# Row statistics of x1 made once in the first node stage of a graph network kernel, and gathered as two table columns

## The chip, the cores and the metric

The kernel runs on one core of a Trainium2 chip. The metric is the device time of one execution in microseconds (us), the median of several runs. PE is the matrix engine, DVE the vector engine, ACT the scalar engine, POOL GpSimd, and SP the engine whose queue issues most DMA transfers.

## The reference, cut to what matters

Four graph layers work on x (10000 x 512) and 5000 edges. The first two, cut to the lines around the change:

```python
def _layernorm(x, axis=-1, eps=1e-05):
    m = jnp.mean(x, axis=axis, keepdims=True)
    v = jnp.var(x, axis=axis, keepdims=True)
    return (x - m) / jnp.sqrt(v + eps)
...
h = jnp.maximum(_layernorm(x, axis=-1), 0.0)
x = x + _L0_gnn_ref(h, ...)      # this x is the kernel's x1
h = jnp.maximum(_layernorm(x, axis=-1), 0.0)
x = x + _L1_gnn_ref(h, edge_index, edge_type_8, edge_weight, ...)
...
# _L0_gnn_ref, node part
z = jnp.concatenate([x, agg], axis=1)
return jax.nn.relu(z @ W3 + b3) @ W4 + b4
...
# _L1_gnn_ref, message part
h = (x @ W.T).reshape(n, h_, d_)
e_src = jnp.einsum('ehd,hd->eh', h[src], a_src)
e_dst = jnp.einsum('ehd,hd->eh', h[dst], a_dst)
```

## The kernel before, in words

The program runs its stages one after the other, each in a block of its own, and each stage's tiles have a letter: prepare (a), layer 0's edges (b), **layer 0's nodes (c)**, **layer 1's messages (d)**, softmax (s) and sums (e), **layer 1's nodes (n)**, and so on up to layer 3's edges (h). Tables in HBM pass the results on; x1 is one, 512 columns wide (its name in the trace is x). A tile has 128 rows, a group four tiles.

**First node stage, c (layer0_nodes).** Ten rounds of two groups, b = 0 and 1. The trace has it from about 948 to 1640 us, a round in some 66 us. Per round: PE turns the normalised rows of X into c_tp_ps; ACT copies them out (c_hTh, L928) and DVE makes the rest of the split (c_hTl, L976). PE multiplies with W3 (c_u_ps); DVE adds the gathered sums (L993, c_U); PE turns that (L1037); ACT applies bias and relu (c_R at L935, c_zh at L936), and DVE subtracts them for c_zl (L983), five chunks per group. PE multiplies with W4 (c_o_ps), and DVE adds the result to the residual in XB (L1003). Each engine's order is written out by hand as one program. While one round runs, the next round's X is loaded (L831) and its statistics made (L963); the residual x is loaded into XB (L841); POOL gathers the sums of edges (L898) and adds the bias b4 to XB in two instructions of 128 x 2048 (L903). The store of XB into x1 (L845) waits for the last addition of its group. SP's queue in a round is: two loads of X, two residual loads, each of which waits for the store of its half of XB a round ago, two stores.

**Messages, d (layer1_messages).** From about 1640 to 1909 us. Ten groups of 4 x 128 edges, each with a source row and a destination row of x1, gathered by POOL into d_X, eight gathers a group (L1160), one group ahead. DVE makes the statistics (L1239, L1246, L1248, L1250), with the root on ACT (L1179), ACT applies them with relu (L86), and PE turns the rows (L1323). ACT and DVE split them (L1195, L1258), PE multiplies with W (d_m_ps) and with the projection of the attention vectors (d_proj_ps), and ACT and DVE copy the messages out (L1199, L1263). The projections' operand is made at the stage's start (L1310).

**Second node stage, n (layer1_nodes).** From about 2034 to 2413 us, ten rounds like c's, without PE: it loads x1 (n_X), makes its statistics on DVE (L1687), adds x1's own rows and the gathered sums (L1708, L1734, L1741), and POOL adds a bias (L1643) and gathers (L1632).

Of the kernel before, what the change touches and what calls it, by code (L numbers as in the profile page):

```python
# [37 lines left out]
EPS = 1e-5  # L38
XW = F + 4
# [751 lines left out]
def layer0_nodes(nc, core, a, keep, T0, x1):  # L791
# [10 lines left out]
    o_ready, o_out = sem("c_o"), sem("c_oout")  # L802
    stored = [sem("c_st0"), sem("c_st1")]
# [3 lines left out]
    with ExitStack() as st:  # L807
        sb = lambda n, s, d=F32: core.sb(st, "c_" + n, s, d)
        X = sb("X", [P, 2, GROUP, F])
        XB = sb("XB", [P, 2, GROUP, F])  # L810
        G = sb("G", [P, 2, GROUP, IN])
        idx = sb("idx", [P, GT], I32)
        stt = core.stats(st, "c")
        hTh, hTl = sb("hTh", [P, 2, KF, GROUP * P], F32R), sb("hTl", [P, 2, KF, GROUP * P], F32R)
# [12 lines left out]
        with nc.Block() as block:  # L827
            @block.sync
            def _(sp):
# [3 lines left out]
                def load_last(buf, b, sems):  # L833

                    for p, n in LAST:
                        at = (NG - 1) * GROUP * P + p * GROUP
                        sp.dma_start(buf[p:p + n, b, :, :], a["x"][at:at + n * GROUP, :].rearrange("(p j) f -> p j f", p=n)
                                     ).then_inc(sems[b], 16)
# [47 lines left out]
            def _(pool):  # L886
# [5 lines left out]
                def round_(r, late):  # L892
# [8 lines left out]
                    for b in range(2):  # L901
                        pool.wait_ge(res_loaded[b], r * 16 + (16 + late * b))
                        pool.tensor_tensor(XB[:, b, :, :], XB[:, b, :, :], over(b4[:, :].unsqueeze(1), [P, GROUP, F]),  # L903
# [10 lines left out]
            def _(act):  # L914
                def root(r):
                    act.wait_ge(var_ready, r * GT + GT)
                    layer_norm_std(act, stt, keep["eps"]).then_inc(std_ready, 1)
                    act.wait_ge(norm_ready, r + 1)

# [24 lines left out]
                with act.Fori(0, NR) as r:  # L944
# [7 lines left out]
                    for j in range(GROUP):  # L952
                        turned_rows(r + 1, (2 * j, 2 * j + 1))

            @block.vector
            def _(dve):
# [41 lines left out]
                def add_residual(r, b, j):  # L998
# [4 lines left out]
                    dve.tensor_tensor(XB[:, b, j, :], o[:, t % 2, :], XB[:, b, j, :], ALU.add).then_inc(o_out, 1)  # L1003

                def round_(r, late):
# [6 lines left out]
                    for j in range(GROUP):  # L1012
# [87 lines left out]
def layer1_messages(nc, core, a, keep, x1, msg, logit):  # L1100
# [5 lines left out]
    x_loaded = [sem("d_x0"), sem("d_x1")]  # L1106
    ln_step, var_ready, std_ready, norm_ready, h_ready = (sem("d_" + n) for n in ("lnstep", "var", "std", "norm", "h"))
# [6 lines left out]
    with ExitStack() as st:  # L1114
        sb = lambda n, s, d=F32: core.sb(st, "d_" + n, s, d)
        X = sb("X", [P, 2, 2, GROUP, F])
        idx = sb("idx", [P, 2, 2 * GROUP], I32)
        stt = core.stats(st, "d")
# [4 lines left out]
        Wraw, Wrow = X[:, 1, 0, :, :], X[:, 1, 1, :, :]  # L1123
# [10 lines left out]
        with nc.Block() as block:  # L1134
# [12 lines left out]
            def _(pool):  # L1147
                pool.memset(diag[:, :, :, :], 0.0).then_inc(diag_set, 1)

                def gather(g, b, before, turned):  # L1150
                    pool.wait_ge(x_loaded[b], before)
# [7 lines left out]
                    for i in range(2 * GROUP):  # L1159
                        pool.indirect_dma_start(X[:, b, i // GROUP, i % GROUP, :], None, x1[:, :],  # L1160
                                                bass.IndirectOffsetOnAxis(idx[:, b, i:i + 1], 0),
                                                bounds_check=ROWS_N - 1, oob_is_err=False).then_inc(x_loaded[b], 16)
# [4 lines left out]
                with pool.Fori(0, ER) as r:  # L1167
                    gather(r * 2 + 1, 1, r * 128, r * 16)
                    gather(r * 2 + 2, 0, r * 128 + 128, r * 16 + 8)
                pool.wait_ge(x_loaded[0], 128 * (ER + 1))  # L1170
                pool.wait_ge(x_loaded[1], 128 * ER)
# [3 lines left out]
            def _(act):  # L1175
                def root(g, q):
                    n = slice(GROUP * q, GROUP * q + GROUP)
                    act.wait_ge(var_ready, g * 8 + (4 * q + 4))
                    act.activation(stt["std"][:, n], stt["mv"][:, n, 1], ACT.Sqrt, bias=keep["eps"][:, 0:1]).then_inc(std_ready, 1)  # L1179

                def norm_rows(g, b, q, rows):
                    act.wait_ge(norm_ready, g * 2 + (q + 1))
                    for j in rows:
                        x = X[:, b, q, j, :]
                        relu_norm(act, x, x, stt, GROUP * q + j).then_inc(h_ready, 1)
# [16 lines left out]
                for q in range(2):  # L1202
                    root(0, q)
# [1468 lines left out]
```

## Time and profile before

| | us |
|---|---|
| median of 3 runs | 3022.01 (3018.73 to 3023.68) |
| span of the profiled execution | 3096.9 |
| first node stage (c) in it | about 948 to 1640 |
| message stage (d) in it | about 1640 to 1909 |
| second node stage (n) in it | about 2034 to 2413 |

No other time of the profiled execution is given; its span is 74.9 us longer than the median.

Rows of the timeline read: start, duration, engine, line, operation, tile written <- tiles read, shapes, how many of them in a row, and in brackets the idle time before them with what ended it. SPq is the issue of a DMA by SP's queue. Rows of stretches read: the stretch, its length, busy time (and instructions) of PE, PE's weight loads, DVE, ACT, POOL, then the granted PE clock (1.00 is 2.4 GHz, 0.50 is 1.2 GHz), the busy share of the DMA engines and GB/s. Rows of waits read: who waited for whom, us in total, how often, the longest.

### The profile page before, as it was taken

Reading aid. Unit: us, or ns where it says so; the run is one execution under the profiler, and the core shown is the slowest. Engines: PE = TensorE matmul, PEld = TensorE weight load, DVE = VectorE, ACT = ScalarE, POOL = GpSimd, SP = SyncE. Lnnn points to the kernel's source line nnn. Section 1 sums busy time; section 2 is a strip of 40 time slices with the busy share of each in tenths; the row PEclk is TensorE's granted clock in tenths of the full one; section 3 lists DMA queues with packets and bytes.
Section 4 is the critical chain, followed back from the end, with each engine's and each line's share of the span. In section 5 each row is a group of like instructions: output and inputs, shape, how many; then the busy total and the mean of one; then the engine's idle time right before and its main releaser. Section 6 shows DMA issues by size and latency. Waiting matters only on the chain. (4 is left out here: it accounts for less than half of the span.)

```text
span 3096.9 us, 40519 instructions
## 1 busy us (share of the span) xinstructions
PE 2274.6 (73%) x13127; PEld 2008.0 (65%) x13127; DVE 1744.5 (56%) x3459; ACT 1089.9 (35%) x1842; POOL 970.3 (31%) x762
## 2 busy tenths in 40 slices
PE   6989999999995999999996996510000165899466
PEld 6979898989895888888885875410000154777355
DVE  4633232323234544445443657879999367999444
ACT  2234333333343343333332554323333263333232
POOL 1001010000003322232313341655665504565565
PEclk9989999999997999999997998765555577999778
DMA  6101010101023232322323231234432534665443
GB/s 200 34 8 55 18 51 17 51 17 50 20 49 145 103 114 95 142 114 94 98 90 123 82 96 42 92 144 146 149 133 101 174 127 178 245 245 222 141 139 119
DMA packets 111202, 330.20 MB, mean 107 GB/s; under 512 B 25980, under 2 KB 39292, under 8 KB 90570
## 3 DMA queue, kind: packets, MB, share of 16 engines
q1 hardware_dynamic: 61628, 228.63, 19.6%
q0 software_dynamic: 42976, 99.20, 10.9%
q10 hardware_dynamic: 6530, 1.53, 0.2%
q8 instruction: 36, 0.59, 0.1%
q14 instruction: 32, 0.26, 0.0%
HBM read 247.80 MB, written 128.41 MB: 121 GB/s over the span
## 5 line engine op out<-in xcount | busy, mean ns | idle before, releaser
L1914 PE MATMUL f_c_ps<-f_zeros 128*40 128x258 f32 x4 | 1.9, 641 | 389.2 <-DVE f_heads L1369 389.2
L1914 PEld LDWEIGHTS f_c_ps<-f_zeros 128*40 128x40 f32 x4 | 0.6, 174 | 390.2 <-DVE f_heads L1369 389.7
L135 PE MATMUL b_y_ps<-W23h,b_Rh 128*128 128x320 f32 x800 | 249.7, 312 | 0.0
L136 PE MATMUL b_y_ps<-W23l,b_Rh 128*128 128x320 f32 x800 | 246.4, 308 | 0.6 <-issue 0.6
L137 PE MATMUL b_y_ps<-W23h,b_Rl 128*128 128x320 f32 x800 | 246.6, 308 | 0.2 <-issue 0.2
L536 POOL DMA_INDIRECT b_X<-in_x,b_idx x40 | 40.3, 1008 | 635.0 <-PE b_tp_ps L716 624.4
L135 PE MATMUL b_hid_ps<-b_hTh,W1h 128*128 128x512 f32 x500 | 201.4, 403 | 7.9 <-ACT b_Rh L585 7.9
L135 PE MATMUL c_u_ps<-c_W3h,c_hTh 128*128 128x320 f32 x640 | 201.2, 314 | 0.0
L136 PE MATMUL b_hid_ps<-b_hTl,W1h 128*128 128x512 f32 x500 | 200.2, 400 | 0.0
L137 PE MATMUL b_hid_ps<-b_hTh,W1l 128*128 128x512 f32 x500 | 200.0, 400 | 0.0
L137 PE MATMUL c_u_ps<-c_W3h,c_hTl 128*128 128x320 f32 x640 | 198.0, 309 | 0.0
L136 PE MATMUL c_u_ps<-c_W3l,c_hTh 128*128 128x320 f32 x640 | 197.9, 309 | 0.0
L903 POOL TENSOR_TENSOR c_XB<-c_XB,c_b 128x2048 f32<-128x2048 f32 x20 | 92.0, 4617 | 325.9 <-DMA c_XB<-in_x 325.9
L650 DVE TENSOR_TENSOR b_Rl<-b_R,b_Rh 128x512 fp32r<-128x512 f32 x100 | 69.2, 692 | 220.8 <-ACT b_Rh L585 220.8
L935 ACT ACTIVATE c_R<-c_tp_ps,c_b 128x512 f32<-128x512 f32 x100 | 68.8, 688 | 305.4 <-PE c_tp_ps L1037 297.4
L135 PE MATMUL c_o_ps<-c_W4h,c_zh 128*128 128x512 f32 x400 | 162.2, 405 | 3.8 <-DVE c_zl L983 3.7
L675 DVE TENSOR_TENSOR b_Yl<-b_y_ps,b_Yh 128x320 fp32r<-128x320 f32 x80 | 39.3, 492 | 216.1 <-ACT b_Yh L597 212.5
L137 PE MATMUL c_o_ps<-c_W4h,c_zl 128*128 128x512 f32 x400 | 156.8, 392 | 0.0
L136 PE MATMUL c_o_ps<-c_W4l,c_zh 128*128 128x512 f32 x400 | 156.3, 391 | 0.0
L137 PEld LDWEIGHTS b_y_ps<-W23h,b_Rl 128*128 128x128 f32 x800 | 150.1, 188 | 1.2 <-issue 1.2
L136 PEld LDWEIGHTS b_y_ps<-W23l,b_Rh 128*128 128x128 f32 x800 | 150.2, 188 | 1.0 <-issue 0.5
L135 PEld LDWEIGHTS b_y_ps<-W23h,b_Rh 128*128 128x128 f32 x800 | 150.2, 188 | 0.5
(383 smaller groups left out, 7238.5 us busy)
## 6 DMA issues: line engine op xcount, KB each, us to landing
c_X<-in_x SPq DMA_DIRECT2D x21, 1024.0 KB
x<-n_O SPq DMA_DIRECT2D x20, 1032.0 KB, 4.0
g_X<-x SPq DMA_DIRECT2D x20, 1032.0 KB
x<-c_XB SPq DMA_DIRECT2D x20, 1024.0 KB, 4.2
n_X<-x SPq DMA_DIRECT2D x20, 1024.0 KB
x<-g_O SPq DMA_DIRECT2D x20, 1024.0 KB, 3.9
c_XB<-in_x SPq DMA_DIRECT2D x19, 1024.0 KB
out<-g_B SPq DMA_DIRECT2D x19, 1024.0 KB
```

Source lines behind the costliest of these rows:

```text
L135: pe.matmul(out, ah, bh, start=first, stop=False)
L136: pe.matmul(out, ah, bl, start=False, stop=False)
L137: return pe.matmul(out, al, bh, start=False, stop=last)
L536: pool.indirect_dma_start(X[:, i // GROUP, i % GROUP, :], None, a["x"][:, :], bass.IndirectOffsetOnAxis(idx[:, i:i + 1], 0), bounds_check= ...
L650: dve.tensor_tensor(Rl[:, m, :], R[:, :], Rh[:, m, :].bitcast(F32), ALU.subtract).then_inc(hid_lo, 1)
L675: dve.tensor_tensor(Yl[:, t % 2, w], y[:, h, 0:HALF], Yh[:, t % 2, w].bitcast(F32), ALU.subtract).then_inc(y_out[h], 1)
L903: pool.tensor_tensor(XB[:, b, :, :], XB[:, b, :, :], over(b4[:, :].unsqueeze(1), [P, GROUP, F]), ALU.add).then_inc(res_ready, 1)
L935: act.activation(R[:, k % 2, :], tp[:, k % 2, :], ACT.Relu, bias=b3[:, c:c + 1]).then_inc(z_hi, 1)
L1914: pe.matmul(c[0:ET, h, 0:HW], zeros[:, 0:ET], zeros[:, :], start=True, stop=False)
```

## The change

x1 becomes 514 columns wide (XV). In stage c, DVE makes for each finished row of XB its mean and variance, ACT the root, and DVE writes 1/root into column 512 and -mean/root into column 513. The store of a group now waits for these. The residual load, POOL's bias addition and DVE's addition work on the first 512 columns of rows 514 wide. In stage d the statistics on DVE and the root on ACT are gone; the gathers fetch 514 columns, and ACT takes scale and bias from the gathered columns. Source rows and destination rows have semaphores of their own, for which ACT waits. Stage n reads 512 of the 514 columns of x1 (group_rows with F), and its code is the same. The diff, cut:

```diff
+XV = F + 2
@@ layer0_nodes
-        XB = sb("XB", [P, 2, GROUP, F])
+        XB = sb("XB", [P, 2, GROUP, XV])
+        one = core.stats(st, "c1")
...
-                    sp.dma_start(XB[:, b, :, :], group_rows(a["x"], g, F)).then_inc(res_loaded[b], 16)
+                    sp.dma_start(XB[:, b, :, 0:F], group_rows(a["x"], g, F)).then_inc(res_loaded[b], 16)
...
-                    sp.wait_ge(o_out, r * GT + (4 * b + 4 + 2))
-                    sp.dma_start(group_rows(x1, g, F), XB[:, b, :, :]).then_inc(stored[b], 16)
+                    sp.wait_ge(x1_ready, r * 2 + (b + 1))
+                    sp.dma_start(group_rows(x1, g, XV), XB[:, b, :, :]).then_inc(stored[b], 16)
...
+                def root1(r, b):
+                    n = slice(GROUP * b, GROUP * b + GROUP)
+                    act.wait_ge(var1_ready, r * GT + (GROUP * b + GROUP))
+                    act.activation(one["std"][:, n], one["mv"][:, n, 1], ACT.Sqrt, bias=keep["eps"][:, 0:1]).then_inc(std1_ready, 1)
...
                     for j in range(GROUP):
                         turned_rows(r + 1, (2 * j, 2 * j + 1))
+                        if j == 0:
+                            root1(r, 0)
+                    root1(r, 1)
...
+                def stats1(r, b, j):
+                    t = GROUP * b + j
+                    dve.wait_ge(o_out, r * GT + (t + 1 + 2))
+                    dve.bn_stats(one["raw"][:, t, :], XB[:, b, j, 0:F]).then_inc(out_step, 1)
+                def mean1(r, b):
+                    dve.wait_ge(out_step, r * 10 + (5 * b + 4))
+                    dve.sem_inc(one["go"], 1)
+                    for i in range(GROUP * b, GROUP * b + GROUP):
+                        dve.bn_aggr(one["mv"][:, i, :], one["raw"][:, i, :]).then_inc(var1_ready, 1)
+                def scale1(r, b):
+                    n = slice(GROUP * b, GROUP * b + GROUP)
+                    dve.wait_ge(std1_ready, r * 2 + (b + 1))
+                    dve.reciprocal(XB[:, b, :, F:F + 1], one["std"][:, n].unsqueeze(2)).then_inc(out_step, 1)
+                    dve.wait_ge(out_step, r * 10 + (5 * b + 5))
+                    dve.scalar_tensor_tensor(out=XB[:, b, :, F + 1:F + 2], in0=one["mv"][:, n, 0:1], scalar=-1.0,
+                                             in1=XB[:, b, :, F:F + 1], op0=ALU.mult, op1=ALU.mult).then_inc(x1_ready, 1)
...
                         add_residual(r, 0, j)
                         hidden(r, 1, Z_SLOT[j])
+                        if j:
+                            stats1(r, 0, j - 1)
                     for j in range(GROUP):
                         add_residual(r, 1, j)
+                        if j == 0:
+                            stats1(r, 0, GROUP - 1)
+                            mean1(r, 0)
                         turned_rows(r + 1, (2 * j, 2 * j + 1))
+                        if j == 0:
+                            scale1(r, 0)
+                        else:
+                            stats1(r, 1, j - 1)
+                    stats1(r, 1, GROUP - 1)
+                    mean1(r, 1)
+                    scale1(r, 1)
@@ layer1_messages
-        X = sb("X", [P, 2, 2, GROUP, F])
+        X = sb("X", [P, 2, 2, GROUP, XV])
...
-                def root(g, q):
-                    n = slice(GROUP * q, GROUP * q + GROUP)
-                    act.wait_ge(var_ready, g * 8 + (4 * q + 4))
-                    act.activation(stt["std"][:, n], stt["mv"][:, n, 1], ACT.Sqrt, bias=keep["eps"][:, 0:1]).then_inc(std_ready, 1)
-                def norm_rows(g, b, q, rows):
-                    act.wait_ge(norm_ready, g * 2 + (q + 1))
+                def norm_rows(b, q, rows, loaded):
+                    act.wait_ge(x_loaded[b][q], loaded)
                     for j in rows:
-                        x = X[:, b, q, j, :]
-                        relu_norm(act, x, x, stt, GROUP * q + j).then_inc(h_ready, 1)
+                        x = X[:, b, q, j, 0:F]
+                        act.activation(x, x, ACT.Relu, bias=X[:, b, q, j, F + 1:F + 2],
+                                       scale=X[:, b, q, j, F:F + 1]).then_inc(h_ready, 1)
...
```

DVE at the end of a round of stage c, the last round, before: second group's additions to XB (L1003) and the splits for the next round (L976).

```order
L1003 TENSOR_TENSOR c_XB<-c_o_ps,c_XB 128x512 x2
L976 TENSOR_TENSOR c_hTl<-c_tp_ps,c_hTh 128x512 x2
L1003 TENSOR_TENSOR c_XB<-c_o_ps,c_XB 128x512
L976 TENSOR_TENSOR c_hTl<-c_tp_ps,c_hTh 128x512 x2
L1003 TENSOR_TENSOR c_XB<-c_o_ps,c_XB 128x512
L976 TENSOR_TENSOR c_hTl<-c_tp_ps,c_hTh 128x512 x2
L1003 TENSOR_TENSOR c_XB<-c_o_ps,c_XB 128x512
L976 TENSOR_TENSOR c_hTl<-c_tp_ps,c_hTh 128x512 x2
```

And DVE at the same place now, from the second group's third addition (L1014 is the addition, L987 the split).

```order
L1014 TENSOR_TENSOR c_XB<-c_o_ps,c_XB 128x512
L987 TENSOR_TENSOR c_hTl<-c_tp_ps,c_hTh 128x512 x2
L1020 BN_STATS c_raw<-c_XB 128x6
L1014 TENSOR_TENSOR c_XB<-c_o_ps,c_XB 128x512
L987 TENSOR_TENSOR c_hTl<-c_tp_ps,c_hTh 128x512 x2
L1020 BN_STATS c_raw<-c_XB 128x6 x2
L1026 BN_AGGR c_mv<-c_raw 128x2 x4
L1032 RECIPROCAL c_XB<-c_std 128x4
L1034 SCALAR_TENSOR_TENSOR c_XB<-c_mv,c_XB 128x4
```

The last addition, the last split pair, two statistics, four aggregates and the two columns now stand in this order; the store waits for the last of them instead of for the last addition.

DVE in the first group of stage d's loop, before (ISA and REGISTER_ALU rows set up addresses).

```order
L1239 BN_STATS d_raw<-d_X 128x6 x4
L1262 ISA
L1263 ISA
L1263 COPY msg<-d_m_ps 128x260
L1257 ISA
L1258 TENSOR_TENSOR d_hTl<-d_tp_ps,d_hTh 128x512
L1257 REGISTER_ALU
L1258 TENSOR_TENSOR d_hTl<-d_tp_ps,d_hTh 128x512
L1243 ISA
L1246 BN_AGGR d_mv<-d_raw 128x2 x4
L1247 ISA
L1248 RECIPROCAL d_rstd<-d_std 128x4
```

And DVE at the same place now (L1284 is the copy of a message, L1279 the split).

```order
L1284 ISA
L1284 COPY msg<-d_m_ps 128x260
L1278 ISA
L1279 TENSOR_TENSOR d_hTl<-d_tp_ps,d_hTh 128x512
L1278 REGISTER_ALU
L1279 TENSOR_TENSOR d_hTl<-d_tp_ps,d_hTh 128x512
L1283 REGISTER_ALU
L1284 ISA
L1284 COPY msg<-d_m_ps 128x260
```

The statistics, which waited for the gather ahead of the first copy, are gone, and so are the aggregates and the reciprocal behind the splits.

## Rows read from the trace of the kernel before

**Rows 1.** The page, busy time: engine, busy us, share, instructions.

```profile
PE 2274.6 (73%) x13127; PEld 2008.0 (65%) x13127; DVE 1744.5 (56%) x3459; ACT 1089.9 (35%) x1842; POOL 970.3 (31%) x762
```

**Rows 2.** Stretches, in the stages c, d and n.

```profile
1150.00:1200.00 50.00, 49.77 (x302) 45.16 (x301) 23.04 (x36) 17.05 (x28) 11.30 (x5) 1.00 0.34 133
1800.00:1850.00 50.00, 45.09 (x333) 39.80 (x332) 29.58 (x80) 28.11 (x53) 16.64 (x20) 0.96 0.29 84
2033.00:2420.00 387.00, 0.01 (x1) 0.01 (x1) 340.68 (x612) 121.23 (x181) 226.54 (x112) 0.50 0.36 131
```

**Rows 3.** Timeline of stage c, DVE and SP's queue at a round's end.

```profile
1173.07 0.69 DVE L1003 TENSOR_TENSOR c_XB<-c_o_ps,c_XB 128x512 f32<-128x512 f32 x1 [1.98 <-PE c_o_ps L137]
1174.13 1.29 DVE L976 TENSOR_TENSOR c_hTl<-c_tp_ps,c_hTh 128x512 fp32r<-128x512 f32 x2 [0.36 <-ACT c_hTh L928]
...
1157.13 17.02 SPq L845 DMA_DIRECT2D x<-c_XB  x2
1174.71 1.65 SPq L831 DMA_DIRECT2D c_X<-in_x  x2
1176.63 2.28 SPq L841 DMA_DIRECT2D c_XB<-in_x  x2
...
1173.79 0.35 SPq L845 DMA_DIRECT2D x<-c_XB  x1
```

**Rows 4.** Stretches: DMA in the loads of stage c, and at its start.

```profile
1178.00:1182.00 4.00, 4.00 (x30) 4.00 (x29) 1.49 (x4) 0.00 (x0) 0.00 (x0) 1.00 1.01 420
957.00:961.00 4.00, 0.00 (x0) 0.00 (x0) 2.08 (x12) 1.64 (x3) 0.00 (x0) 0.50 1.04 398
```

**Rows 5.** Waits and timeline, stage c: POOL's additions, c_zl on DVE, PE's transposes.

```profile
POOL c_XB L903 <- DMA c_XB<-in_x: 314.5, 9, 36.4
...
1186.33 9.18 POOL L903 TENSOR_TENSOR c_XB<-c_XB,c_b 128x2048 f32<-128x2048 f32 x2 [34.51 <-DMA c_XB<-in_x]
...
1193.28 3.38 DVE L983 TENSOR_TENSOR c_zl<-c_R,c_zh 128x512 fp32r<-128x512 f32 x2 [0.63 <-ACT c_zh L936]
...
1198.68 1.28 DVE L983 TENSOR_TENSOR c_zl<-c_R,c_zh 128x512 fp32r<-128x512 f32 x2
...
1196.12 1.26 PE L1037 MATMUL c_tp_ps<-ident,c_U 128*128 128x128 f32 x8 [0.21 <-DVE c_zl L983]
1200.73 0.60 PE L1037 MATMUL c_tp_ps<-ident,c_U 128*128 128x128 f32 x4
...
1592.87 1.26 PE L1037 MATMUL c_tp_ps<-ident,c_U 128*128 128x128 f32 x8 [1.27 <-DVE c_zl L983]
```

**Rows 6.** Timeline of stage n: POOL and DVE.

```profile
2093.69 9.58 POOL L1643 TENSOR_TENSOR n_X<-n_X,n_beta 128x2048 f32<-128x2048 f32 x2 [14.81 <-ACT n_H L86]
...
2112.80 9.20 POOL L1632 DMA_INDIRECT n_G<-T,n_idx  x1 [0.30 <-issue]
...
2094.54 4.38 DVE L1708 SCALAR_TENSOR_TENSOR n_G<-n_G,has,n_H 128x512 f32<-128x512 f32 x1
2098.84 0.68 DVE L1713 BATCH_NORM_STATS2 n_raw<-n_G 128x6 f32<-128x512 f32 x1
2099.45 4.38 DVE L1708 SCALAR_TENSOR_TENSOR n_G<-n_G,has,n_H 128x512 f32<-128x512 f32 x1
```

**Rows 7.** Timeline of stage d's start: PE's projections and DVE's statistics.

```profile
1655.10 13.82 PE L1310 MATMUL d_proj_ps<-d_diag,d_X 128*128 128x8 f32 x64 [19.56 <-DMA d_diag<-in_L_gnn_a_dst]
...
1655.35 2.47 DVE L1239 BATCH_NORM_STATS2 d_raw<-d_X 128x6 f32<-128x512 f32 x4 [18.31 <-DMA d_X<-x,d_idx]
...
1658.93 0.16 DVE L1250 SCALAR_TENSOR_TENSOR d_shift<-d_mv,d_rstd 128x4 f32<-128x4 f32 x1
```

**Rows 8.** Timeline of stage d, first group.

```profile
1684.34 2.47 DVE L1239 BATCH_NORM_STATS2 d_raw<-d_X 128x6 f32<-128x512 f32 x4 [9.69 <-DMA d_X<-x,d_idx]
...
1687.79 1.97 PE L1323 MATMUL d_tp_ps<-ident,d_X 128*128 128x128 f32 x8 [6.00 <-DVE d_hTl L1258]
```

**Rows 9.** Stretch behind that wait.

```profile
1688.00:1692.00 4.00, 4.00 (x23) 4.00 (x23) 1.70 (x9) 2.91 (x6) 1.01 (x1) 0.63 0.03 6
```

**Rows 10.** Stretch in a later stage's gathers of 2064-byte rows.

```profile
2428.00:2432.00 4.00, 0.00 (x0) 0.00 (x0) 2.14 (x4) 0.00 (x0) 3.09 (x4) 0.50 0.73 205
```

**Rows 11.** Waits of stage d between 1675 and 1905 us.

```profile
PE d_m_ps L135 <- DVE d_hTl L1258: 7.3, 9, 1.2
...
PE d_proj_ps L135 <- DVE d_hTl L1258: 2.6, 10, 0.5
```

More of the change, by code:

```diff
@@ L802, in layer0_nodes @@
     o_ready, o_out = sem("c_o"), sem("c_oout")
+    out_step, var1_ready, std1_ready, x1_ready = (sem("c1_" + n) for n in ("step", "var", "std", "x1"))
     stored = [sem("c_st0"), sem("c_st1")]
@@ L902, in round_ @@
                         pool.wait_ge(res_loaded[b], r * 16 + (16 + late * b))
-                        pool.tensor_tensor(XB[:, b, :, :], XB[:, b, :, :], over(b4[:, :].unsqueeze(1), [P, GROUP, F]),
+                        pool.tensor_tensor(XB[:, b, :, 0:F], XB[:, b, :, 0:F], over(b4[:, :].unsqueeze(1), [P, GROUP, F]),
                                            ALU.add).then_inc(res_ready, 1)
@@ L1105, in layer1_messages @@
     idx_staged, go = sem("d_idx"), sem("d_go")
-    x_loaded = [sem("d_x0"), sem("d_x1")]
-    ln_step, var_ready, std_ready, norm_ready, h_ready = (sem("d_" + n) for n in ("lnstep", "var", "std", "norm", "h"))
+    x_loaded = [[sem(f"d_x{b}{n}") for n in ("src", "dst")] for b in range(2)]
+    h_ready = sem("d_h")
     tp_ready, tp_free, hT_hi = sem("d_tp"), sem("d_tpfree"), sem("d_hThi")
@@ L1150, in gather @@
                 def gather(g, b, before, turned):
-                    pool.wait_ge(x_loaded[b], before)
+                    for q in range(2):
+                        pool.wait_ge(x_loaded[b][q], before)
                     pool.sem_inc(go, 1)
@@ L1167, in _ @@
                 with pool.Fori(0, ER) as r:
[L1168 to L1171, printed above, removed]
+                    gather(r * 2 + 1, 1, r * 64, r * 16)
+                    gather(r * 2 + 2, 0, r * 64 + 64, r * 16 + 8)
+                for q in range(2):
+                    pool.wait_ge(x_loaded[0][q], 64 * (ER + 1))
+                    pool.wait_ge(x_loaded[1][q], 64 * ER)
                 pool.sem_inc(go, 1)
@@ L1202, in _ @@
                 for q in range(2):
-                    root(0, q)
-                    norm_rows(0, 0, q, range(GROUP))
+                    norm_rows(0, q, range(GROUP), 64)
                 split_on_act(act, Wraw[:, :, :], Wh[:, :, 0:F], w_loaded, 16 * 18, w_hi)
@@ L1226, in _ @@
                         turned(g + 1, 1 - b, 0, (0, 1), g * 4)
-                        root(g + 1, 1)
                         message(g, 3)
                         turned(g + 1, 1 - b, 0, (2, 3), g * 4)
-                        norm_rows(g + 1, 1 - b, 1, range(GROUP))
+                        norm_rows(1 - b, 1, range(GROUP), loaded)
             @block.vector
             def _(dve):
-                def stats(b, q, loaded):
-                    if q == 0:
-                        dve.wait_ge(x_loaded[b], loaded)
-                    for j in range(GROUP):
-                        dve.bn_stats(stt["raw"][:, GROUP * q + j, :], X[:, b, q, j, :]).then_inc(ln_step, 1)
-                def scale(g, q):
-                    n = slice(GROUP * q, GROUP * q + GROUP)
-                    dve.wait_ge(ln_step, g * 10 + (5 * q + 4))
-                    dve.sem_inc(stt["go"], 1)
-                    for i in range(GROUP * q, GROUP * q + GROUP):
-                        dve.bn_aggr(stt["mv"][:, i, :], stt["raw"][:, i, :]).then_inc(var_ready, 1)
-                    dve.wait_ge(std_ready, g * 2 + (q + 1))
-                    dve.reciprocal(stt["rstd"][:, n], stt["std"][:, n]).then_inc(ln_step, 1)
-                    dve.wait_ge(ln_step, g * 10 + (5 * q + 5))
-                    dve.scalar_tensor_tensor(out=stt["shift"][:, n], in0=stt["mv"][:, n, 0], scalar=-1.0, in1=stt["rstd"][:, n],
-                                             op0=ALU.mult, op1=ALU.mult).then_inc(norm_ready, 1)
                 def turned(g, b, q, chunks):
@@ L1277, in logits @@
                                       ALU.mult).then_inc(dot_read, 1)
-                for q in range(2):
-                    stats(0, q, 128)
-                    scale(0, q)
                 split_on_dve(dve, Wraw[:, :, :], Wh[:, :, 0:F], Wl[:, :, 0:F], w_hi, 1, w_lo)
@@ L2580, in program @@
         T0 = table("T0", ROWS_E, IN, 1)
-        x1 = table("x1", ROWS_N, F, 2)
+        x1 = table("x1", ROWS_N, XV, 2)
         T1 = table("T1", ROWS_T, F, 3)
```

23 lines of the change are left out of this document (9 added, 14 removed).

## The prediction, made before the changed kernel was run

> **What bounds the kernel now.** I read the page's busy times first, then the table of stretches, then each engine's timeline in one round of the two stages that the change touches, then the table of waits. The page gives PE 73% of the span and DVE 56% [rows 1], but the stretches say more: in the first node stage PE is busy 49.77 of 50 us with DVE at 23.04, in the message stage PE 45.09 of 50 with DVE at 29.58, and in the second node stage DVE is busy 340.68 of 387 with PE idle [rows 2]. So DVE work is free in the first stage unless it delays something that PE waits for. DVE work taken out of the message stage is worth only the PE waits that it ends. The profiled span is 3096.9 us, the median 3022.01, 74.9 us less. I sum against the span and take the same 74.9 off. What counts as no change is 0.2%, 6.0 us.
>
> **First node stage: the added work itself.** Per round of two groups there are 8 row statistics, 8 aggregates, 2 reciprocals, 2 small products on DVE and 2 roots on ACT. Priced by the same operations of the message stage (4 statistics 2.47 us, then 1.27 us from the end of the last one at 1657.82 to the end of the shift at 1659.09, aggregate, root on ACT and reciprocal included [rows 7]), that is 2 x 3.74 = 7.5 us per round of some 66 us, over ten rounds 75 us. DVE has 27 of 50 us idle there [rows 2]; while a statistic stands ahead of a c_hTl pair it delays that pair by 0.6 to 1.2 us, and PE asks for it over 2 us later. Cost 0.
>
> **The store, and what is queued behind it.** The last addition of a round starts at 1173.07 and the store of that group is issued at 1173.79, by the end of a row that begins at 1157.13 and lasts 17.02 us [rows 3]. Afterwards the store waits for the shift column. DVE does its c_hTl pair first (1174.13 to 1175.42 [rows 3]), then two statistics (half of 2.47, 1.2 us), then the 1.27 us tail [rows 7]: 1177.9. The store is late by **4.1 us**. On SP's queue the two loads of X and the two residual loads stand behind it [rows 3], and the second residual load also waits until the store has landed. All four move by 4.1 us. The residual load now writes 2048-byte pieces into rows of 2056 bytes. Contiguous, DMA moves 420 GB/s [rows 4]; pieces of about that size moved 398 GB/s [rows 4]. Over the 2 MB of a round that is 5.0 against 5.3 us, +0.3; the bounds are 0 and +1.5. Together POOL's two bias additions, which wait for these loads in nine rounds [rows 5], start **4.5 us later** (4.1 to 5.6).
>
> **Where POOL's additions now fall.** Today the pair runs from 1186.33 to 1195.51 [rows 5]. DVE's first two c_zl (both inputs in SBUF) are issued at 1193.28 and take 3.38 us instead of the 1.28 of the next two: they end only after POOL's pair. PE goes on at 1196.12, 0.6 us after POOL, having waited 0.21 [rows 5]. In the tenth round the lead is smaller and PE waits 1.27 [rows 5]. So these two engines exclude each other here, an instruction at a time, and PE is within 0.2 us of feeling it. Moved by 4.5 us, the first addition ends at 1186.33 + 4.5 + 4.59 = 1195.4, where the pair ends today, and the second one is still to run for 4.59. What matters is who gets in at 1195.4.
> In the second node stage the same collision can be seen: POOL's pair of 9.58 us, during which one DVE product takes 4.38 us, and the next, after one statistic (no second SBUF input), again 4.38 [rows 6]. One DVE instruction gets through between two of POOL's. And where DVE has 14 such instructions one right behind the other, POOL's own instruction of 1 us took 9.20 us, until DVE's row of them ended [rows 6]. Read together: DVE gets in at the boundary and keeps what it holds over instructions that follow each other directly. Then both first c_zl go at 1195.4 and end at 1196.65, as today. POOL's second addition runs 1196.65 to 1201.25, in DVE's statistics, and blocks the next c_zl (1198.68 today). PE wants that for its transposes at 1200.73 [rows 5] and gets it at 1201.25 + 0.65 = 1201.9. PE waits 1.17 us more in each of nine rounds: **+10.5 us**. At a shift of 4.1 us it is 0.6 a round (+5), at 5.6 some 2.8 (+25).
> The Trainium skill's page "SBUF — State Buffer" (section "SBUF: two separate sides") says that the port pair which DVE and GpSimd share is an exclusive lock for the whole instruction, and that a DVE instruction with two SBUF inputs contends with a GpSimd instruction that reads SBUF. The 3.38 and 4.38 us above agree. It says further that whichever starts first gets the pair; POOL's second addition is ready before the second c_zl starts, so by the page POOL would run between the two. That is rival B, and the 9.20 us row speaks against it.
>
> **End of the first stage.** Nothing follows the last store there but the next stage, so the delay shows whole: **+4.1 us**.
>
> **Message stage, its start.** The gather is followed by 64 PE products from 1655.10 to 1668.92, which wait for the diagonals' loads [rows 7]. DVE's statistics from 1655.35 and ACT's normalisation stand beside them, and the weight split that follows on ACT ends before PE does. What is removed was hidden, and the start moves by the cost of the wider gathers alone. These are 2056 bytes a row; a later stage gathers rows of 2064 bytes at 205 GB/s with DMA busy 0.73 [rows 10], so POOL's issues set the pace. Taken +0.3, bounds 0 and +1.
>
> **Group 0.** DVE waits 9.69 us for the gather, 2.47 us of statistics follow, and behind them stands a c_hTl of the group before, which releases PE: PE waits **6.00 us** [rows 8], and then works at 0.63 of its clock [rows 9]. Afterwards DVE has nothing of the gather in its queue. The wait goes (6.0), and so do the 4 us at 0.63 of the clock (4 x 0.37 = 1.5). ACT now waits for the four source rows itself, but only before its first normalisation, and these gathers are issued first. **-7.5 us** (-6 to -9).
>
> **The other nine groups.** PE waits for d_hTl before the projection 2.6 us in ten groups, and before a message product 7.3 us in nine [rows 11]. The first stands right behind statistics on DVE and goes: **-2**. The second follows a late copy of a message, which is late only while a gather is in flight, and statistics do not stand ahead of it, so I leave it. Bounds 0 and -12.
>
> **Second node stage.** Its loads of x1 become 2048-byte pieces too. They are issued two rounds ahead, and DVE is the bound [rows 2]: 0, but POOL and DVE collide there as above, so a shift of a microsecond can fall either way, plus or minus 5.
>
> **Sum.** +10.5 + 4.1 + 0.3 - 7.5 - 2.0 = +5.4. Span 3096.9 + 5.4 = 3102.3, less 74.9: **3027 us**.
>
> **Rivals.**
> A, the forecast: 3027, its own range 3016 to 3042 from the bounds above.
> B, slower: at 1195.4 DVE's first c_zl gets in, and POOL's second addition takes the pair between it and the second one. The second c_zl then starts at 1196.05 + 4.59 = 1200.6 and PE, which wants it at 1196.7, goes on at 1201.3: 4.6 us per round. After its wait of 6.00 us PE ran at 0.63 of its clock for 4 us [rows 9], 1.5 us lost, so some 6 us per round, 54 in nine. 54 + 4.1 + 0.3 - 9.5 = +48.9: 3071 (3058 if the clock holds). It decides as soon as POOL's pair starts less than 4.6 us ahead of the first c_zl; today it is 1193.28 - 1186.33 = 6.95, afterwards 2.4. For it: one DVE instruction only is seen to pass between two of POOL's [rows 6]. Against it: the 9.20 us row.
> C, better than forecast: the 7.3 us of message waits [rows 11] and the dots' gaps around them do come from a DVE queue that will be 6 us a group shorter; they go, some -10. 3017. For it: DVE is at 29.58 of 50 there, 13 us in a group of 22, and loses about 6 of them. Against it: no statistics directly ahead of the waits.
> D, the store's delay doesn't reach POOL, because loads have slack on DMA: 10.5 us less, 3016.5. DMA at 420 GB/s without a gap between the load issues and POOL's start [rows 4, 5] speaks against it, so it has a part of C's chance.
>
> **How the numbers follow.** A 0.54, B 0.22, C and D 0.24. Range 3010 to 3068: below it both C and D at once, or C with the whole of the message stage's bound (0.08), above it B's upper half (0.11). A's centre lies just inside no change, and a shift on POOL of 0.3 us more takes it out: of A's 0.54, same 0.33, slower 0.16, faster 0.05. C and D lie at the lower edge: faster 0.16, same 0.08. B is slower. Together faster 0.21, same 0.41, slower 0.38.
>
> **What would show it.** In the first node stage: the store issued about 4 us after the last addition, POOL's pair beginning near 4.5 us later against PE's round, a first c_zl pair of about the same 3.4 us and a later c_zl of 2 to 4 us (A), or one c_zl of 4.6 after another (B), with PE waits of 1.2 or 4.6. In the message stage: no 6.00 us wait in group 0, periods of about 22 us afterwards. The forecast is wrong if POOL's second addition doesn't fall on the third c_zl, or if the groups of the message stage shorten towards the 20 us of the last.

## The result, and the profile after

The changed kernel takes **3055.16 us** (3049.23 to 3063.84, 4 runs) against 3022.85 before: 1.0114 of before, with an interval of 1.0087 to 1.0141. It is slower by 32 us, where +5 had been forecast as the likeliest case. What came is the mechanism of rival B.

One thing has to be said about the base first. The profiled execution of before that is shown ahead of the prediction ran some 75 us longer than the median. A second profile of the same kernel has a span of 3022.9. By stage, from the first instruction of one stage to that of the next, in us:

| stage | before, 1st profile | before, 2nd profile | after | after less 2nd |
|---|---|---|---|---|
| c, first nodes | 692.3 | 685.6 | 737.1 | +51.5 |
| d, messages | 268.7 | 243.4 | 226.2 | -17.2 |
| s and e | 125.4 | 125.4 | 126.5 | +1.1 |
| n, second nodes | 383.4 | 384.5 | 378.1 | -6.4 |
| f, edges of layer 2 | 136.4 | 112.0 | 112.1 | +0.1 |
| g | 331.4 | 331.9 | 332.8 | +0.9 |
| h | 211.0 | 191.8 | 192.0 | +0.2 |

The stages f and h have the same code in both kernels, and the first profile is long by 24 and 19 us in them and by 25 in d. All "less 2nd" figures add up to the 29.3 us between the spans 3022.9 and 3052.2 when the start is counted (-0.9). From here on, after is compared with the second profile.

The page of after, busy times, answers to [rows 1]:

```profile
PE 2261.5 (74%) x13127; PEld 2004.4 (66%) x13127; DVE 1772.2 (58%) x3439; ACT 1090.7 (36%) x1840; POOL 957.3 (31%) x762
```

PE's busy time hardly moved. What moved is when it stands still. The timeline of after at the end of one round of stage c (DVE, then SP's queue) answers to [rows 3]:

```profile
1180.91 0.69 DVE L1014 TENSOR_TENSOR c_XB<-c_o_ps,c_XB 128x512 f32<-128x512 f32 x1 [1.38 <-PE c_o_ps L138]
1181.96 1.29 DVE L987 TENSOR_TENSOR c_hTl<-c_tp_ps,c_hTh 128x512 fp32r<-128x512 f32 x2 [0.36 <-ACT c_hTh L936]
1183.17 1.28 DVE L1020 BATCH_NORM_STATS2 c_raw<-c_XB 128x6 f32<-128x512 f32 x2
1184.60 0.38 DVE L1026 BATCH_NORM_AGGREGATE c_mv<-c_raw 128x2 f32<-128x6 f32 x4 [0.15 <-DVE c_raw L1020]
1185.34 0.18 DVE L1032 RECIPROCAL c_XB<-c_std 128x4 f32<-128x4 f32 x1 [0.36 <-ACT c_std L926]
1185.56 0.17 DVE L1034 SCALAR_TENSOR_TENSOR c_XB<-c_mv,c_XB 128x4 f32<-128x4 f32 x1
...
1171.48 14.76 SPq L848 DMA_DIRECT2D x<-c_XB  x2
1186.80 1.65 SPq L834 DMA_DIRECT2D c_X<-in_x  x2
1188.71 2.57 SPq L844 DMA_DIRECT2D c_XB<-in_x  x2
```

The second store's issue ends at 1171.48 + 14.76 = 1186.24, which is 5.3 us after the start of the last addition; before it was 1.1 (1157.13 + 17.02 - 1173.07). It is late by 4.2. The four loads stand behind it. The same round of after, POOL, DVE and PE at the first c_zl, answers to [rows 5]:

```profile
1198.66 8.80 POOL L906 TENSOR_TENSOR c_XB<-c_XB,c_b 128x2048 f32<-128x2048 f32 x2 [38.70 <-DMA c_XB<-in_x]
...
1201.11 6.89 DVE L994 TENSOR_TENSOR c_zl<-c_R,c_zh 128x512 fp32r<-128x512 f32 x2 [0.63 <-ACT c_zh L944]
...
1208.06 0.66 PE L1081 MATMUL c_tp_ps<-ident,c_U 128*128 128x128 f32 x4 [3.90 <-DVE c_zl L994]
```

POOL's first addition takes 4.2 us and ends at 1202.9. The two c_zl together take 6.89 us (before 3.38). A view of that line alone gives the longer of the two:

```profile
L994 DVE TENSOR_TENSOR c_zl<-c_R,c_zh x4: 678/1498/4649, 1201.1 to 1210.6; 128x512 fp32r<-128x512 f32 x4
```

So the first waits 1.7 us and runs (2.3), then the second is held for POOL's whole second addition (4.65), and PE stands for 3.90 us. The second c_zl takes 4.64 to 4.65 us in all nine rounds from the second on. The periods between the first c_zl of two rounds, counted from the second round, are 69.9 to 70.3 us and the last one 71.9, where the second profile of before has 64.8 to 65.1 and 66.2. The clock after that wait, from the table of stretches:

```profile
1204.00:1208.00 4.00, 0.16 (x2) 0.00 (x0) 4.00 (x2) 1.26 (x2) 4.00 (x2) 1.00 0.00 0
1208.00:1212.00 4.00, 3.94 (x20) 3.95 (x21) 4.00 (x9) 1.26 (x2) 0.05 (x1) 0.68 0.00 0
1212.00:1216.00 4.00, 4.00 (x28) 3.99 (x27) 1.98 (x4) 1.26 (x2) 0.00 (x0) 0.90 0.00 0
```

0.68 and 0.90 of full clock over 4 us each cost 4 x 0.32 + 4 x 0.10 = 1.7 us. With 3.90 us of wait that makes 5.6, less the few tenths that PE already waited before.

In the message stage the wait of group 0 is gone. First PE in the second profile of before, then PE in after at the same place, where only the stage's start still has waits:

```profile
1681.49 1.97 PE L1323 MATMUL d_tp_ps<-ident,d_X 128*128 128x128 f32 x8 [5.66 <-DVE d_hTl L1258]
```

```profile
1700.12 13.82 PE L1324 MATMUL d_proj_ps<-d_diag,d_X 128*128 128x8 f32 x64 [24.73 <-DMA d_diag<-in_L_gnn_a_dst]
1716.36 1.97 PE L1337 MATMUL d_tp_ps<-ident,d_X 128*128 128x128 f32 x8 [0.61 <-DVE d_hTl L1279]
```

From the stage's start to the fourth message of group 0 it is 60.3 us before and 52.5 after, -7.8. The nine periods that follow add up to 178.1 before (19.4 to 19.9, the last 21.6) and 168.7 after (18.74 to 18.76 each), -9.4.

### The profile page after: what moved, and what is told of

Its sections match the earlier page's. It is cut to its first block and busy times, and to the rows that moved or that the text cites. A ratio compares the mean times of both kernels' runs of the same rounds, so it can differ in the third digit from the quotient of the medians.

```text
span 3052.2 us, 40494 instructions
## 1 busy us (share of the span) xinstructions
PE 2261.5 (74%) x13127; PEld 2004.4 (66%) x13127; DVE 1772.2 (58%) x3439; ACT 1090.7 (36%) x1840; POOL 957.3 (31%) x762
## 5 line engine op out<-in xcount | busy, mean ns | idle before, releaser
L136 PE MATMUL c_u_ps<-c_W3h,c_hTh 128*128 128x320 f32 x640 | 207.4, 324 | 0.0
```

What stands on the lines that cost most here:

```text
L136: pe.matmul(out, ah, bh, start=first, stop=False)
```

## The experiments

**The halves.** *before_again* is the kernel before, profiled once more.

> The kernel before, profiled once more. By stage, the first profile of it has c 692, d 269, n 383, f 136, h 211 us, and the changed kernel c 737, d 226, n 378, f 112, h 192. The stages f and h are the same code in both, yet differ by 24 and 19. Theory 1 (the first profiled execution was a long one in the stages that gather rows, by the 75 us that its span stood above the median): this span is near 3021, with c 692, f 112, h 192 and d about 235 to 240, so that the change is worth some 10 in d. Theory 2 (d really gained 42): d is near 269 again and the span near 3097, and the median of +32 is then unexplained.

Measured 3024.61 us, span 3022.9, the stages as in the table above: theory 1, and d 243.4.

*c_part_alone* keeps the change in c and puts the statistics of d back:

```diff
 # layer1_messages of the changed kernel, with before's DVE and ACT work
+                for q in range(2):
+                    stats(0, q, 128)
+                    scale(0, q)
...
+                        stats(1 - b, 0, r * 128 + 128 * (b + 1))
+                        scale(g + 1, 0)
```

> The first stage's half of the change alone: statistics and columns made in c, store late, table 514 wide; stage d makes its own statistics again, on 514-wide rows. Theory 1 (POOL's second addition now stands between the first and the second c_zl in each of nine rounds): c 737 as in the changed kernel, time +40 to +48 over before. Theory 2 (most of the loss is elsewhere, in wider gathers or in n): +5 to +20.

1.0161 of before (1.0143 to 1.0179), +49 us. c 740.0, d 244.4: theory 1, a little above its range.

*d_part_alone* does the opposite:

```diff
 # layer0_nodes of the changed kernel
-                        if j:
-                            stats1(r, 0, j - 1)
...
-                    sp.wait_ge(x1_ready, r * 2 + (b + 1))
+                    sp.wait_ge(o_out, r * GT + (4 * b + 4 + 2))
...
+                pool.memset(XB[:, :, :, F:F + 1], 1.0).then_inc(init, 1)
+                pool.memset(XB[:, :, :, F + 1:F + 2], 0.0).then_inc(init, 1)
```

> The message stage's half alone: c makes no statistics, the two columns hold 1 and 0 from the start (so layer 1's rows aren't normalised in the messages, relu alone is applied), and the store waits for the last addition as before; residual load and additions work on 514-wide rows. Theory 1: c within 2 us of 692, total 8 to 15 faster than before, by the wait in group 0 and small ones. Theory 2: 30 to 42 faster, as the two profiles' d stages differ.

0.9922 of before (0.9906 to 0.9939), -23 us; c 683.7, d 225.4. By stages d gave 18.0 and c 1.9. More than theory 1 had, less than theory 2: the message half is worth 18 us. The strided 514-wide rows cost c nothing. Both halves together explain the whole: c +54 and d -18 here, +51.5 and -17.2 in the changed kernel.

**Delay or work.** *store_late* is before with only the second store moved:

```diff
                 def store(r, g, b):
-                    sp.wait_ge(o_out, r * GT + (4 * b + 4 + 2))
+                    if b:
+                        sp.wait_ge(late_go, r + 2)
+                    else:
+                        sp.wait_ge(o_out, r * GT + (4 * b + 4 + 2))
...
 # DVE, after the first addition of gathered sums of a round
+                    if b == 0 and j == 0:
+                        dve.wait_ge(o_out, r * GT + 2)
+                        dve.sem_inc(late_go, 1)
```

> Before, with one thing changed: the second store of each round of c waits until DVE has made the first addition of gathered sums of the next round, which is 4 to 4.5 us after the last addition to XB. No added statistics, no wider rows. Theory 1 (the delay of the loads behind the store moves POOL's pair into c_zl): c longer by 35 to 45, with one c_zl of 4.6 in nine rounds, and PE waits of 3 to 4 us each. Rival (the added DVE work or the strided rows do it, not the delay): within 5 us of before.

1.0150 of before (1.0133 to 1.0167), c 736.5. Its timeline, POOL, DVE and PE:

```profile
1196.71 9.53 POOL L906 TENSOR_TENSOR c_XB<-c_XB,c_b 128x2048 f32<-128x2048 f32 x2 [38.39 <-DMA c_XB<-in_x]
...
1199.46 7.32 DVE L986 TENSOR_TENSOR c_zl<-c_R,c_zh 128x512 fp32r<-128x512 f32 x2 [0.63 <-ACT c_zh L939]
...
1206.84 1.12 PE L1045 MATMUL c_tp_ps<-ident,c_U 128*128 128x128 f32 x4 [4.26 <-DVE c_zl L986]
```

A late store alone gives the loss of c. c was 51 us longer, more than the 35 to 45 expected, since the clock's fall had not been counted into that, and it fell behind each of the nine waits.

*work_alone* is the counterpart: all of c's added work on DVE and ACT, and no delay. It leaves out that the statistics are of XB: they are made of a constant tile, and nobody reads them.

```diff
+                def stats1(r, b, j):
+                    t = GROUP * b + j
+                    dve.wait_ge(o_out, r * GT + (t + 1 + 2))
+                    dve.bn_stats(one["raw"][:, t, :], W4h[:, t % KI, :].bitcast(F32)).then_inc(out_step, 1)
...
 # mean1, root1, scale1 at their new places, into tiles of their own; store waits for o_out
```

> The kernel before plus the added DVE and ACT work of c alone: statistics, aggregates, roots, reciprocals and products at their new places, but of a constant 128x512 tile and into tiles that nobody reads; the store waits for the last addition as before, and rows are 512 wide. Theory 1: it costs nothing, c 684 to 688, within 3 us of before. Rival (DVE's work delays c_hTl or c_zl and takes part in the 51 us): 5 to 20 slower.

0.9996 of before (0.9982 to 1.0011), c 685.4: the work costs nothing.

**What decides the collision.** *columns_earlier* shortens the delay to half, 2.1 us:

```diff
                     for j in range(GROUP):
+                        if j == GROUP - 1:
+                            stats1(r, 1, j - 1)
                         add_residual(r, 1, j)
...
+                        if j == GROUP - 1:
+                            stats1(r, 1, j)
+                            mean1(r, 1)
+                            scale1(r, 1)
                         turned_rows(r + 1, (2 * j, 2 * j + 1))
...
-                    stats1(r, 1, GROUP - 1)
-                    mean1(r, 1)
-                    scale1(r, 1)
```

> The changed kernel with the last two statistics of a round, the aggregates and the two columns written before the last c_hTl pair instead of behind it, so the second store is late by about 2.1 us instead of 4.2. POOL's pair then starts 4.8 to 5.1 us ahead of the first c_zl instead of 2.5. Theory 1 (what decides is which POOL instruction is running when the first c_zl comes; the first one takes 4.2 us): the second addition is already running, both c_zl wait for its end in one piece (about 3.9 us in place of 2.3 and then 4.65), PE waits 1.5 to 2 us a round instead of 3.9, c 698 to 706. Rival (the cost grows evenly with the delay, or the delay costs by itself): c 711 and a second long c_zl in each round.

1.0041 of before (1.0026 to 1.0055), c 711.8. In seven rounds the c_zl behaved as theory 1 had it: one of 4.3 to 4.5 us and no second long one, with POOL's pair starting 4.4 to 4.6 us ahead. In the last two rounds the pair started 3.3 and 3.9 us ahead, the first addition was still running, and the second c_zl took 4.67 and 4.36 us. The last round, POOL and DVE:

```profile
1596.60 8.82 POOL L906 TENSOR_TENSOR c_XB<-c_XB,c_b 128x2048 f32<-128x2048 f32 x2 [37.30 <-DMA c_XB<-in_x]
...
1600.45 0.92 DVE L994 TENSOR_TENSOR c_zl<-c_R,c_zh 128x512 fp32r<-128x512 f32 x1 [0.66 <-ACT c_zh L944]
1601.61 4.36 DVE L994 TENSOR_TENSOR c_zl<-c_R,c_zh 128x512 fp32r<-128x512 f32 x1 [0.24 <-ACT c_zh L944]
```

The price, c 711.8, was the rival's. PE in a round of the first half and in one of the second half, and the four microseconds of clock behind each:

```profile
1195.90 1.26 PE L1084 MATMUL c_tp_ps<-ident,c_U 128*128 128x128 f32 x8 [1.89 <-DVE c_zl L994]
```

```profile
1399.38 1.25 PE L1084 MATMUL c_tp_ps<-ident,c_U 128*128 128x128 f32 x8 [1.99 <-DVE c_zl L994]
```

```profile
1196.00:1200.00 4.00, 4.00 (x29) 3.82 (x30) 4.00 (x8) 2.43 (x4) 0.00 (x0) 1.00 0.00 0
...
1400.00:1404.00 4.00, 4.00 (x19) 4.00 (x19) 4.00 (x8) 2.42 (x4) 0.00 (x0) 0.58 0.00 0
```

Three rounds with waits of 1.77 to 1.89 us kept the clock at 1.00, and their periods are 66.6 to 66.7 us. Behind the waits of the next four rounds, 1.93 to 1.99 us, it fell each time (to 0.58 over the four microseconds shown), and their periods are 68.3. So 1.6 us a round is the clock, which neither theory had in its number.

*zl_joined* takes away the gap between the two c_zl and leaves the late store:

```diff
                 def hidden(r, b, chunks):
+                    if b == 0 and chunks == (0, 1):
+                        dve.wait_ge(z_hi, r * (4 * KI) + 4)
+                        dve.tensor_tensor(zl[:, 0, 0:2, :], R[:, :, :], zh[:, 0, 0:2, :].bitcast(F32),
+                                          ALU.subtract).then_inc(tp_free, 2)
+                        return
```

> The changed kernel with the first two c_zl of a round made by one DVE instruction of 128x1024, so POOL has no place between them; the store is as late as in the changed kernel. Theory 1 (the loss is POOL's second addition getting the port between the first and the second c_zl): the joined instruction comes 3.7 us behind the start of POOL's pair, waits 0.5 us for the first addition, runs, and POOL's second addition holds up the third c_zl instead, for which PE waits about 1.2 us, as the forecast had it. PE waits 1 to 2 us a round instead of 3.9, c 695 to 710, ratio to before 0.999 to 1.004. Rival (POOL's instructions, ready first, both go ahead of DVE's, or the loss isn't in the gap between the two): the joined c_zl waits 4.7 us or more, and c stays near 737, ratio 1.011.

**0.9970 of before** (0.9958 to 0.9982), c 692.1, below the range expected. POOL and DVE:

```profile
1185.86 9.37 POOL L906 TENSOR_TENSOR c_XB<-c_XB,c_b 128x2048 f32<-128x2048 f32 x2 [38.76 <-DMA c_XB<-in_x]
...
1189.48 1.67 DVE L993 TENSOR_TENSOR c_zl<-c_R,c_zh 128x1024 fp32r<-128x1024 f32 x1 [1.86 <-ACT c_zh L944]
...
1193.20 3.17 DVE L999 TENSOR_TENSOR c_zl<-c_R,c_zh 128x512 fp32r<-128x512 f32 x2
```

This is the forecast's picture: the joined c_zl comes 3.6 us behind the start of the pair, waits for the first addition to end, gets in ahead of the second, and POOL's second addition holds up the third c_zl instead. PE had work queued for most of that; its wait stays at 0.35 us in this round (1.8 and 1.0 in the last two), and the clock at 1.00 through all rounds. The joined instruction also comes later, since it waits for two c_zh. That isn't what saves it: in the ninth round it comes 2.2 us behind the start of POOL's pair, closer than the 2.45 of the changed kernel, and still runs ahead of the second addition:

```profile
1513.32 9.40 POOL L906 TENSOR_TENSOR c_XB<-c_XB,c_b 128x2048 f32<-128x2048 f32 x2 [40.16 <-DMA c_XB<-in_x]
...
1515.53 3.12 DVE L993 TENSOR_TENSOR c_zl<-c_R,c_zh 128x1024 fp32r<-128x1024 f32 x1 [1.89 <-ACT c_zh L944]
```

One DVE instruction instead of two turns a loss of 32 us into a gain of about 9.

**Cures.** *add_split* cuts each addition in four:

```diff
-                        pool.tensor_tensor(XB[:, b, :, 0:F], XB[:, b, :, 0:F], over(b4[:, :].unsqueeze(1), [P, GROUP, F]),
-                                           ALU.add).then_inc(res_ready, 1)
+                        for j in range(GROUP):
+                            pool.tensor_tensor(XB[:, b, j, 0:F], XB[:, b, j, 0:F], b4[:, :], ALU.add).then_inc(res_ready, 1)
```

> The changed kernel with each of POOL's two bias additions of 128x2048 in c cut into four of 128x512 (about 1.1 us each), at the same place. Theory 1 (the lock holds for one instruction, and POOL's next one gets in behind each c_zl): a c_zl is held for 1.2 us at most, PE waits 0.5 to 1.5 us a round instead of 3.9, total 3018 to 3030. Rival (whoever has a run of instructions keeps the port, as POOL's 9.20 us in the n stage suggested for DVE): the second c_zl still waits for all that is left of POOL's, 4 us, total 3045 to 3060.

0.9926 of before (0.9902 to 0.9950), median 2994.23, c 684.8. The c_zl behave as theory 1 had it, and the time is below its range. POOL and DVE:

```profile
1188.77 11.03 POOL L907 TENSOR_TENSOR c_XB<-c_XB,c_b 128x512 f32<-128x512 f32 x8 [38.66 <-DMA c_XB<-in_x]
...
1191.28 3.13 DVE L994 TENSOR_TENSOR c_zl<-c_R,c_zh 128x512 fp32r<-128x512 f32 x2 [0.63 <-ACT c_zh L944]
...
1196.43 2.42 DVE L994 TENSOR_TENSOR c_zl<-c_R,c_zh 128x512 fp32r<-128x512 f32 x2
```

POOL's 8 pieces last 11.03 us in all and leave DVE in between each time: four c_zl take 5.55 us instead of 2.56, and none waits for more than one piece.

*residual_early* changes SP's order:

```diff
+                with sp.Fori(0, NR - 3) as r:
+                    store(r, r * 2, 0)
+                    sp.wait_ge(stored[0], r * 16 + 16)
+                    residual(r * 2 + 2, 0)
+                    sp.wait_ge(tp_ready, r * TPR + (TPR + 2 * KF))
+                    for b in range(2):
+                        load(r * 2 + (4 + b), b)
+                    store(r, r * 2 + 1, 1)
+                    sp.wait_ge(stored[1], r * 16 + 16)
+                    residual(r * 2 + 3, 1)
```

> The changed kernel with SP's queue in c in another order: the residual load of each half is issued as soon as that half's store has landed, so the first half's stands ahead of the two loads of X, and the second's directly behind its own store. The statistics, the late store and the 514-wide rows stay. Theory 1 (the loss is the collision of POOL's second addition with c_zl): POOL's additions end before the first c_zl, all c_zl take 0.7 us, c falls from 737 to about 689 (the 4 us at the stage's end stay), d stays at 226, total 3003 to 3010, faster than before by 15 to 20. Rival (the late store costs by something else, or the added DVE work does): c stays above 710 and the total above 3030.

0.9924 of before (0.9902 to 0.9945), c 683.6, d 225.6, median 2997.29: theory 1, and again below its range. Its POOL:

```profile
1172.91 4.23 POOL L915 TENSOR_TENSOR c_XB<-c_XB,c_b 128x2048 f32<-128x2048 f32 x1 [20.94 <-DMA c_XB<-in_x]
1189.54 4.23 POOL L915 TENSOR_TENSOR c_XB<-c_XB,c_b 128x2048 f32<-128x2048 f32 x1 [12.40 <-DMA c_XB<-in_x]
```

The first addition starts 20.2 us ahead of the first c_zl. The second ends at 1193.8, 0.7 us behind the start of that c_zl, and the pair of c_zl takes 1.85 us.

The same cures on the kernel before, as controls: *before_residual_early*

> The kernel before with the same order of SP's queue in c, without the change. Theory 1: POOL's additions leave c_zl alone, which cost PE 0 to 1.3 us a round, so c is 1 to 4 us shorter and the total 3019 to 3025. If it gains 10 or more, the order of the queue has a worth of its own, and the gain of residual_early isn't the message stage's.

0.9966 (0.9950 to 0.9981), c 679.8, and *before_add_split*

> The kernel before with POOL's additions in c cut in four, without the change. add_split was 0.9926 of before. Theory 1: cutting them is worth little by itself, 0 to 6 us (ratio 0.998 to 1.0), and the rest of add_split's gain is the message stage's 17. Rival: the cut is worth 12 or more by itself (0.996 or less), in c or by its effect on the n stage.

0.9978 (0.9963 to 0.9992), c 678.8. Their c is 6 to 7 us shorter than before's, where 1 to 4 had been expected for the first: the collision cost the kernel before that much, and the wait of 1.27 us in the tenth round [rows 5] was part of it. The whole gain of before_residual_early is 0.34%, about 10 us, which is where its expectation had put a worth of the queue's order by itself. Its profile is 5.8 us shorter in c, and 13.0 in the second node stage, whose length varies without any change in its code (below). So a worth of the order beyond c is neither shown nor excluded. *all_three* has both cures and the earlier columns:

> The changed kernel with the three cures together: residual loads issued as soon as the halves are stored, additions cut in four, columns written before the last c_hTl pair. Theory 1: POOL's additions all end before the first c_zl or hold it for 1 us at most, the end of c is late by 2 us instead of 4; c 678 to 682, d 225, 3 to 6 us better than residual_early or add_split, ratio to before 0.990 to 0.992.

0.9928 (0.9911 to 0.9945), c 682.7, n 384.6. It is not better than either cure alone by anything that these intervals can tell. The change with one cure is worth about 0.75% over before and some 0.4 to 0.5% over before with the same cure. That is what the stages say: 17.2 us won in d less 4.2 lost at the end of c are 13 us, 0.43%.

## Why the prediction was right or wrong, point by point

**The store's delay** was right: 4.1 forecast, 4.2 measured. **The end of stage c** was right: after the last round's collision is taken off (10.2 us more from the last round's first c_zl to the next stage, less the 4.9 to 5.7 by which the periods grew), 4.5 to 5.3 us stay for the 4.1 forecast. Between residual_early and before_residual_early, where PE has no such waits, c differs by 3.8.

**POOL's additions** came as close to c_zl as forecast: 2.45 us ahead, 2.4 had been said. In the rounds two to eight they start 17.7 to 17.9 us behind the last addition of the round before, where it was 13.0 to 13.3: 4.6 us later for the 4.5 forecast, of which 4.2 are the store's delay. The strided rows have their part in the small rest, and POOL's addition is shorter in them, 4.2 us instead of 4.6. **The added work** was forecast at nothing, and work_alone measured nothing.

**The step that failed** is the one that chose between A and B: "DVE gets in at the boundary and keeps what it holds over instructions that follow each other directly." The first half holds, the second doesn't. It rested on POOL's row of 9.20 us [rows 6], which is the issue of a gather beside 14 DVE instructions in a row. POOL's addition is another kind of instruction, and it gets in between two c_zl: 4.65 us for the second c_zl in after, 4.98 to 5.01 in store_late, and 1.67 for both when they are one instruction. The rows of the second node stage that show additions [rows 6] spoke for B, as the prediction says under B, and had been given less weight. In these rows the two engines take turns, an instruction each. B's price of 54 us for nine rounds was 47 (51.5 less 4.2): PE waited 3.90 us a round where 4.6 had been forecast.

**The number.** The measured 3055 lies in the range of 3010 to 3068, and it does so by the share that B had in that range; the forecast's own case ended at 3042. B's number was 3071 with the clock's part, 16 too many. By the stages of the profiles B's price was 7 too high, the message stage gave 8 more and the second node stage 6. The other stages and the difference between profiles and medians take 5 back. B without the clock, 3058, is nearer only by luck, for the clock did fall. Both signs that the prediction had named for being wrong came: POOL's second addition didn't fall on the third c_zl, and the groups of the message stage shortened, to 18.75 us.

The Trainium skill's page "SBUF — State Buffer" (section "SBUF: two separate sides") says that whichever of the two instructions starts first holds the shared pair of ports for the whole instruction. The trace agrees with it: the second c_zl took 4.65 us. The case that followed from this rule had been given the smaller chance.

**The clock** in B's sum was sized right: 1.5 us a round forecast, 1.7 measured.

**Group 0 of the messages**: -7.5 forecast, -7.8 measured. **The other nine groups**: -2 forecast, -9.4 measured. The mis-sized term is the removal of PE's waits behind statistics. The trace that was read had periods of 21.8 to 23.4 us, and in it most waits stood at other places than in the second profile, where this one alone is 7.8 us in ten groups:

```profile
PE d_proj_ps L135 <- DVE d_hTl L1258: 7.8, 10, 1.7
```

against 2.6 in [rows 11]. Rival C had some 10 us more in this stage than the forecast. 8 more came, though not by the waits that C named. PE's 7.3 us of message waits that the prediction left standing [rows 11] are not in the second profile at all. They belonged to the long execution, and the worth of the change could not be read from them.

**The offset.** The prediction took 74.9 us off the span as if they were spread evenly. They lay in the stages d, f and h (69 of 74). A span of 2.5% above the median was a reason to doubt single rows of a stage, and above all of the stage that the change touched.

**The second node stage**: 0 with plus or minus 5 forecast, -6.4 measured, and nothing shows that this is the change's doing (below).

**Two bounds** of POOL's term don't come out of the rows that the prediction names: at a shift of 4.1 us the same working gives 0.8 us a round and not 0.6, at 5.6 us it gives 2.3 and not 2.8. Nothing above hangs on them.

## What to carry to other kernels

A store that waits a little longer delays every load behind it on its queue; follow that to the instruction that the load releases, and look what will then be running beside it. Where DVE (two SBUF inputs) and POOL work at the same time in short and long instructions, assume that they take turns one instruction at a time: a pair of short ones waits for a long one in the middle, and one joined DVE instruction, shorter POOL pieces or an earlier load removes it. Price such a wait with the clock that PE loses behind it. Before reading small waits, compare the profiled span with the median, and take a second profile if they differ by more than the effect that is looked for.

## What the runs showed of the hardware that had not been expected

**The clock fell behind waits of 1.93 to 1.99 us and not behind waits of 1.77 to 1.89 us**, in the same kernel at the same place (0.58 against 1.00 over the 4 us shown). What makes the difference isn't settled by these seven cases. It made 1.6 us a round.

**POOL's addition of 128x2048 took 4.21 us on rows 514 wide and 4.61 on rows 512 wide**, both without a wait on DVE (first addition of each pair). Its cause wasn't tried.

**The second node stage takes one of a few lengths, which go with the number of long gather issues.** POOL's gather issue of 9.2 us [rows 6] occurs four times in the second profile of before and three times in after. Over the profiles the stage took 364.2 us with one such row (add_split), 371.5 to 371.9 with two (three kernels), 378.1 with three (two kernels, the changed one among them) and 383.4 to 385.0 with four (six profiles): about 6.5 us each. Two others don't fit the row: 386.3 with five, and 378.6 with seven. DVE's waits for those gathers, in the second profile of before and in add_split:

```profile
DVE n_G L1708 <- DMA n_G<-T,n_idx: 26.4, 5, 6.1
```

```profile
DVE n_G L1722 <- DMA n_G<-T,n_idx: 6.8, 2, 4.6
```

The code of the stage is the same in all of them. What sets the number of these rows is open, and of any comparison of two profiles here 6 us, one such row, may be due to it. Stage b, whose code is also the same in all, took 930.8 to 937.4 us over the fourteen profiles. That is why the stages c and d are compared above, and not only the totals. The 6 us that the changed kernel seems to win in that stage come with one such row less.
